# Choice sums moved into the first expert stage, normalisations given to ScalarE, and exponent differences given to TensorE

## The chip, the cores and the metric
The kernel runs on one core of a Trainium2 chip. The metric is the device time of one execution in microseconds (us). All data are float32 unless said otherwise.

## The reference
4096 rows (64 sequences of 64 positions) of 256 features pass through four residual steps, each behind a tanh gate:

```
x = x + tanh(g_xattn[0]) * attention(layernorm(x), ctx)          # 16 x 16 heads within a position
x = x + tanh(g_ffn[0])   * experts0(layernorm(x))                # 16 experts, 6 chosen, plus a shared one
x = x + tanh(g_xattn[1]) * wkv(layernorm(x) as keys, ctx as values)
x = x + tanh(g_ffn[1])   * experts1(layernorm(x))                # 64 experts, 8 chosen
```

The third step, the mixing, is a recurrence over the 64 positions for each feature, with w the decay and u the bonus:

```
no = max(o, u + k); A = exp(o - no); E = exp(u + k - no); y = (A*p + E*v) / (A*q + E)
no2 = max(w + o, k); A2 = exp(w + o - no2); E2 = exp(k - no2); p, q, o = A2*p + E2*v, A2*q + E2, no2
```

## The kernel before
The 4096 rows are 32 tiles of 128 rows, in 8 groups (NG) of four tiles (GT). x_res holds all rows on chip. Each engine has a program of its own, in order, and the engines meet at semaphores and at the ends of the stages A, B, G0, H0, M, H1, I1 (end_stage: every engine drains and waits for all).

- A and B are the attention, G0 the first routing. G0 writes each normalised row once for each chosen expert to a DRAM table (xs_a), sorted by expert.
- H0 (`experts(L0)`, `slots(L0)`) runs 208 tiles of 128 sorted rows through their experts. At step j TensorE turns the rows of tile j, multiplies tile j-1 by its first weights (L920), turns the hidden rows of tile j-2 (L928) and multiplies tile j-3 by the second weights (L937). VectorE adds the bias of tile j-1 (h_gu, L1649), waits for ScalarE's gate (h_sg, L1153), multiplies (h_h, L1655), scales tile j-3 (h_y, L1664), and in every fourth step compares, picks and places the row numbers. GpSimd scatters h_y to y_a, where the six results of a row lie side by side.
- M (`over_time` and what stands around it) does in group order: sum the six results of each row (`choices_summed` on TensorE, L978, from k_a loaded by SyncE, `choices_added` on VectorE, L1735), the statistics (`moments_of`), normalise to keys (`keys`, L1747), turn them, a scan over time for the largest exponent (`exponents`, L1762), the maximum (L1764), four differences (L1765 to L1769), their exponentials on ScalarE (`decays`, L1212 to L1214), scans and products (`over_time`, twice, for the two halves of the features, called chunks), the division (`divided`, L1796, L1801), the residual (`residual`, L1806), and the second routing (`normalised_rows`, `less_largest`, `chosen_experts`, `slots_of`), which lags one group behind. GpSimd issues 32 indirect transfers a group (L646), once `slots_of` has given their rows. The order of all this on each engine is written out by hand in loops over g = 0..8. SyncE loads weights of the second layer behind the last choices (`weights1`).
- H1 is like H0, for 320 tiles of the second layer. From step 103 on it also sums the eight results of rows already done, in four parts at four consecutive steps for a token tile (`token_in` on SyncE, `add_token` on VectorE, L1680 to L1689); a token tile follows every 8 steps. I1 does this for the last group.

The steps at which sums stand come from a table that is made when the kernel is built:

```
sum_at = {}
for t in range(NT - GT):
    ready = tiles_of_groups(t // GT + 1) + SUM_ROOM
    sum_at[t] = ready + (8 if t // GT < NG - 2 else 6) * (t % GT)
```

Of the kernel before, what the change touches and what calls it, by code (L numbers as in the profile page):

```python
# [69 lines left out]
def flamingo(nc, x, ctxT, gates, wqkvT, bqkv, woT, bo, gate0T, gate0b, exp0, exp0b, sh1T, sh3T, sh2T, shb, bs2,  # L70
# [10 lines left out]
    with ctx:  # L81
# [106 lines left out]
        with ExitStack() as st:  # L188
# [19 lines left out]
            h_gu = s_("h_gu", [P, 2, 2 * L0.H])  # L208
            w_bias = s_("w_bias", [P, L0.E * 2 * L0.H])
# [4 lines left out]
        with ExitStack() as st:  # L214
# [8 lines left out]
            w_o = s_("w_o", [P, GB, SEQ + 1])  # L223
            w_t = s_("w_t", [P, KC, 4, GB, SEQ])
# [4 lines left out]
            w_max = s_("w_max", [P, GB, SEQ])  # L229
# [7 lines left out]
            k_a = s_("k_a", [P, 2, GT // 2, L0.K * D])  # L237
# [94 lines left out]
        wk_e = sem("wk_e")  # L332
# [7 lines left out]
        wk_std = sem("wk_std")  # L340
        wk_xn = sem("wk_xn")
        wk_tr = sem("wk_tr")
        wk_k = sem("wk_k")
        k_in = [sem(f"k_in{s}") for s in range(2)]
# [15 lines left out]
        logit_bank = {"a": 2, "b": 6}  # L360
        rank_bank = {"a": 3, "b": 7}
        done = {"a": 0, "b": NG}

        def tiles_of_groups(n):
            return NTOK // NG * L1.K // P * n + L1.E - 1
# [20 lines left out]
        def _(sp):  # L386
# [106 lines left out]
            def token_in(t):  # L493
                if t % GT == 0:
                    n = tiles_of_groups(t // GT + 1)
                    for s in range(YB):
                        sp.wait_ge(lay["b"]["y_st"][s], 16 * ((n - s + YB - 1) // YB))
# [10 lines left out]

            def token_out(t):
                sp.dma_start(out_v[t], s_x[:, t % 2]).then_inc(out_st, 16)  # L510

            def slots(L):
# [5 lines left out]
                if L is L1:  # L518
                    for t, step in sum_at.items():
                        load_at.setdefault((step - SUM_ROOM + 3) // HB + nb - 1, []).append(t)  # L520
                n = L.tiles // HB
                for m in range(max(n, max(load_at, default=0) + 1)):
# [5 lines left out]
                    for t in load_at.get(m, []):  # L528
                        token_in(t)
# [5 lines left out]

            def choices_in(g):
                for h in range(2):
                    if g:
                        sp.wait_ge(k_done, 2 * g - 1 + h)
                    sp.dma_start(k_a[:, h], y_of[g, :, 2 * h:2 * h + 2, 0:L0.K * D]).then_inc(k_in[h], 16)  # L540
# [11 lines left out]
            choices_in(0)  # L552
# [3 lines left out]
            choices_in(1)  # L556
            context_in(1)
            sp.dma_start(e_g1[:], gate1T.rearrange("(c p) n -> p c n", p=P)).then_inc(gate1_in, 16)
            for g in range(NG):
                if g + 2 < NG:  # L560
                    choices_in(g + 2)
# [4 lines left out]
            sp.wait_ge(k_done, 2 * NG)  # L566
            weights1(weight_parts[0])
# [134 lines left out]
        def _(pe):  # L702
# [269 lines left out]
            def choices_summed(g):  # L972
                for h in range(2):
                    pe.wait_ge(k_in[h], 16 * g + 16)
                    if g:
                        pe.wait_ge(k_used, g)
                    for k in range(L0.K):
                        m = pe.matmul(ps[:, 2 + h, :], ident[:], k_a[:, h, :, k * D:(k + 1) * D],  # L978
                                      start=(k == 0), stop=(k == L0.K - 1))
                    m.then_inc(k_done, 1)  # L980
# [18 lines left out]
            choices_summed(0)  # L999
            keys_turned(0)  # L1000
            pe.wait_ge(gate1_in, 16)
            for g in range(NG + 1):
                if g:
                    states_back(g - 1)
                if g + 1 < NG:
                    choices_summed(g + 1)
                if g:
                    turned(L1, g - 1)
                    logits(L1, g - 1, e_g1)
                    ranks(L1, g - 1)  # L1010
                if g + 1 < NG:
                    keys_turned(g + 1)
            experts_of_tiles(L1, 2)
# [7 lines left out]
        def _(act):  # L1021
# [177 lines left out]
            def key_deviations(g):  # L1199
                act.wait_ge(wk_var, g + 1)  # L1200
                part = slice(g * GT, g * GT + GT)
                act.activation(rstd[:, part], mean_v[:, part], ACT.Sqrt).then_inc(wk_std, 1)

# [6 lines left out]
            def decays(g, c):  # L1210
                act.wait_ge(wk_t, 2 * g + c + 1)
                act.activation(w_a2[:, c, :, 1:SEQ + 1], w_t[:, c, 0], ACT.Exp, bias=w_wu[:, c:c + 1])  # L1212
                act.activation(w_e2[:, c, :, 1:SEQ + 1], w_t[:, c, 1], ACT.Exp)
                act.activation(w_ex[:, c].rearrange("p j b t -> p (j b t)"),  # L1214
                               w_t[:, c, 2:4].rearrange("p j b t -> p (j b t)"), ACT.Exp).then_inc(wk_e, 1)

            key_deviations(0)
            act.wait_ge(wk_pad, 1)
            keys_turned(0)
            act.wait_ge(wk_in, 32)  # L1220
            for g in range(NG + 1):
                if g < NG:
                    decays(g, 0)
                if g:
                    deviations(L1, g - 1)
                if g < NG:
                    decays(g, 1)
                if g:
                    turned(L1, g - 1)
                    exponentials_of(L1, g - 1)  # L1230
                if g + 1 < NG:
                    key_deviations(g + 1)
# [8 lines left out]
        def _(dve):  # L1241
# [112 lines left out]
            def moments_of(g, ready=None):  # L1354

                part = slice(g * GT, g * GT + GT)
                for t in range(g * GT, g * GT + GT):
                    dve.bn_stats(stats[:, t, :], x_res[:, t, :])
                dve.drain()
# [260 lines left out]
            def experts(L):  # L1620
# [48 lines left out]
                for t, step in sum_at.items():  # L1669
                    for part in range(4):  # L1670
                        adds_at.setdefault(step + part, []).append((t, part))

# [19 lines left out]
                def body(b, first):  # L1692
# [3 lines left out]
                    for s in range(TD):  # L1696
# [14 lines left out]
                        if L is L1:  # L1711
                            for t, part in adds_at.get(j, []):
                                add_token(t, part)
# [19 lines left out]
            def choices_added(g):  # L1733
# [181 lines left out]
```

## Time and profile before
| | us |
|---|---|
| median of 3 runs | 2300.85 (2299.5 to 2301.25) |
| the profiled execution | 2299.31, its span 2297.5 |
| TensorE matmul busy | 1661.1 (72%) |
| VectorE busy | 1335.5 (58%) |
| ScalarE busy | 688.2 (30%) |
| GpSimd busy | 1051.2 (46%) |
| mean granted clock | 0.856 of full |

The times of rows are in us from the start of the span. H0 goes from about 683 to 1230 us, M from 1230 to 1755, H1 from 1755 to 2270. Busy shares are means over stages with different limits, so each stage is to be read by itself. "Idle before" is the time that an engine stood still in front of an instruction, with the one that released it.

### The profile page before, as it was taken

How to read it: one execution, taken by the hardware profiler on the slowest of the kernel's cores; microseconds unless marked ns; L12 is line 12 of the kernel's file. 1: busy time of each engine (PE TensorE's matmuls, PEld its weight loads, DVE VectorE, ACT ScalarE, POOL GpSimd, SP SyncE). 2: the span in 40 equal slices, each digit the busy share in tenths (PEclk: the TensorE clock that was granted, in tenths of full speed). 3: DMA queues.
4: the chain of work that ended last, by engine and by line, in shares of the span. 5: the costliest groups of instructions: out<-in, count | busy, mean ns of one | idle time of the engine just before them, and what ended most of it. 6: DMA issues, size and time to landing. Idle time of an engine off the chain costs nothing. (4 is left out here: it accounts for less than half of the span.)

```text
span 2297.5 us, 36021 instructions
## 1 busy us (share of the span) xinstructions
PE 1661.1 (72%) x9250; PEld 1209.0 (53%) x9250; DVE 1335.5 (58%) x3716; ACT 688.2 (30%) x1894; POOL 1051.2 (46%) x1039
## 2 busy tenths in 40 slices
PE   2959984987609999999994433333113999999993
PEld 1437763654307777777772222222113888787872
DVE  5113323666505555555552999999951567777774
ACT  1421221222003333333330322222202555455541
POOL 5022001677743333333331056666674666566662
PEclk9989995998859999999996766666556999999997
DMA  4585736533435576675524344442595668788885
GB/s 145 183 147 71 95 68 225 203 122 113 149 128 187 185 257 207 222 239 189 190 84 144 128 139 159 160 162 96 192 339 171 189 193 268 258 279 275 291 270 180
DMA packets 245364, 419.25 MB, mean 182 GB/s; under 512 B 92097, under 2 KB 176193, under 8 KB 243265
## 3 DMA queue, kind: packets, MB, share of 16 engines
q1 hardware_dynamic: 172336, 215.58, 33.1%
q0 software_dynamic: 48144, 138.57, 16.3%
q10 hardware_dynamic: 24704, 62.98, 7.9%
q8 instruction: 78, 1.28, 0.2%
q14 instruction: 102, 0.83, 0.1%
HBM read 253.36 MB, written 209.88 MB: 202 GB/s over the span
## 5 line engine op out<-in xcount | busy, mean ns | idle before, releaser
L920 PE MATMUL ps<-w_all,h_xT 128*128 x2112 | 547.7, 382 | 5.1 <-ACT h_xT L1143 5.1
L937 PE MATMUL ps<-w_all,h_hT 89*128 (+1 forms) x1472 | 416.2, 387 | 2.5
L663 POOL DMA_INDIRECT y_b<-h_y,h_ix x320 | 316.5, 989 | 203.9 <-DVE h_y L1664 105.9
L646 POOL DMA_INDIRECT xs_b<-h_x,slot_of x256 | 270.9, 1058 | 243.8 <-DVE slot_of L1497 167.9
L920 PEld LDWEIGHTS ps<-w_all,h_xT 128*128 128x128 f32 x2112 | 344.2, 191 | 53.9 <-issue 9.4
L663 POOL DMA_INDIRECT y_a<-h_y,h_ix x208 | 201.3, 968 | 350.8 <-DVE h_y L1664 341.6
L913 PE MATMUL ps<-ident,h_x 128*128 128x128 f32 x1056 | 204.6, 275 | 119.4 <-DMA h_x<-xs_a 63.6
L1664 DVE TENSOR_SCALAR h_y<-ps,h_sum 128x256 f32<-128x256 f32 x528 | 253.5, 480 | 49.0 <-PE ps L937 24.9
L937 PEld LDWEIGHTS ps<-w_all,h_hT 89*128 89x128 f32 (+1 forms) x1472 | 239.1, 191 | 32.5 <-issue 7.1
L1143 ACT COPY h_xT<-ps 128x256 f32<-128x256 f32 x528 | 195.8, 371 | 166.9 <-PE ps L913 148.3
L913 PEld LDWEIGHTS ps<-ident,h_x 128*128 128x128 f32 x1056 | 149.2, 142 | 176.5 <-issue 120.1
L646 POOL DMA_INDIRECT xs_a<-h_x,slot_of x192 | 189.4, 986 | 106.0 <-issue 57.9
L928 PE MATMUL ps<-ident,h_h 128*88 128x128 f32 (+1 forms) x736 | 170.3, 278 | 11.4 <-DVE h_h L1655 8.8
L1153 ACT ACTIVATE h_sg<-h_gu 128x176 f32<-128x176 f32 x208 | 72.8, 350 | 324.5 <-DVE h_gu L1649 324.5
L1158 ACT COPY h_hT<-ps 96x128 f32<-96x128 f32 (+1 forms) x528 | 154.3, 292 | 14.1 <-PE ps L928 9.3
L1649 DVE TENSOR_TENSOR h_gu<-ps,w_bias 128x352 f32<-128x352 f32 x208 | 109.0, 524 | 80.8 <-PE ps L920 57.8
L928 PEld LDWEIGHTS ps<-ident,h_h 128*88 128x88 f32 (+1 forms) x736 | 91.0, 124 | 92.8 <-issue 40.1
L1655 DVE TENSOR_TENSOR h_h<-ps,h_sg 128x96 f32<-128x96 f32 x320 | 81.6, 255 | 94.7 <-ACT h_sg L1153 91.5
L1655 DVE TENSOR_TENSOR h_h<-h_gu,h_sg 128x176 f32<-128x176 f32 x208 | 71.1, 342 | 107.1 <-ACT h_sg L1153 107.1
L861 PE MATMUL ps<-h_y,e_w 128*128 128x512 f32 (+1 forms) x192 | 98.1, 666 | 27.4 <-DVE e_h L1569 27.1
L978 PE MATMUL ps<-k_a,ident 128*128 128x512 f32 x192 | 95.7, 660 | 19.2 <-DMA k_a<-y_a 19.2
L1153 ACT ACTIVATE h_sg<-ps 128x96 f32<-128x96 f32 x320 | 80.1, 250 | 94.2 <-PE ps L920 93.7
(237 smaller groups left out, 2143.9 us busy)
## 6 DMA issues: line engine op xcount, KB each, us to landing
xs_b<-void_d ACTq DMA_DIRECT2D x40, 1128.0 KB, 13.7
h_x<-xs_b SPq DMA_DIRECT2D x80, 564.0 KB, 7.6
h_x<-xs_a SPq DMA_DIRECT2D x52, 564.0 KB, 4.2
k_a<-y_a SPq DMA_DIRECT2D x16, 1536.0 KB, 7.9
w_all<-in_exp SPq DMA_DIRECT2D x7, 2560.0 KB
h_x<-y_b SPq DMA_DIRECT2D x28, 512.0 KB, 4.7
s_b<-y_b SPq DMA_DIRECT2D x28, 512.0 KB
qkv_d<-a_out ACTq DMA_DIRECT2D x8, 1536.0 KB, 7.5
```

Source lines behind the costliest of these rows:

```text
L646: pool.indirect_dma_start(xs_d[L.name], bass.IndirectOffsetOnAxis(ap=slot_of[:, g * GT + j, k:k + 1], axis=0), h_x[:, g % NB, j, :], None) ...
L663: pool.indirect_dma_start(y_d[L.name], bass.IndirectOffsetOnAxis(ap=h_ix[:, s:s + 1], axis=0), h_y[:, s % YB, :], None).then_inc(q["y_st"] ...
L913: m = pe.transpose(ps[:, s % 2, c * P:(c + 1) * P], h_x[:, i // HB % nb, s % HB, c * P:(c + 1) * P], ident[:])
L920: m = pe.matmul(ps[:, 2 + s % 2, 0:2 * L.H], h_xT[:, s % 2, c, :], w_all[:, bass.ds(e * L.W + c * 2 * L.H, 2 * L.H)], start=(c == 0), stop ...
L928: m = pe.transpose(ps[0:h1, 4 + s % 2, j * P:(j + 1) * P], h_h[:, s % 2, j * h1:(j + 1) * h1], ident[:])
L937: m = pe.matmul(ps[:, 6 + s % 2, 0:D], h_hT[0:w, s % 2, j, :], w_all[0:w, bass.ds(e * L.W + L.up0 + j * D, D)], start=(j == 0), stop=(j == ...
L1143: act.copy(h_xT[:, s % 2].rearrange("p c n -> p (c n)"), ps[:, s % 2, 0:D])\
L1153: act.activation(h_sg[:, s % 2, 0:L.H], src, ACT.Silu).then_inc(q["s_done"], 1)
L1158: act.copy(h_hT[0:h1, s % 2, 0:L.NC, :].rearrange("p j n -> p (j n)"), ps[0:h1, 4 + s % 2, 0:L.NC * P]).then_inc(q["ht_ready"], 1)
L1649: dve.tensor_tensor(h_gu[:, s % 2, :], ps[:, 2 + s % 2, 0:2 * L.H], w_bias[:, bass.ds(e * 2 * L.H, 2 * L.H)], ALU.add).then_inc(q["b_done" ...
L1655: dve.tensor_tensor(h_h[:, s % 2, 0:L.H], src, h_sg[:, s % 2, 0:L.H], ALU.mult)\
L1664: dve.tensor_scalar(h_y[:, s % YB, :], ps[:, 6 + s % 2, 0:D], h_sum[:, s // HB, s % HB, 0:1], None, ALU.mult)\
```

## The change
1. The choice sums of the first seven groups (28 token tiles) leave M and go into H0: SyncE loads a token tile's six results (h_c) between the row loads, and VectorE adds them in parts at consecutive steps. With the last tile of a group the moments follow. The token tiles stand 6 steps apart, in the last of the seven groups 4. The last group is summed in M as before, from a k_a loaded at once.
2. In M, `keys` and the four multiplications of `normalised_rows` leave VectorE. ScalarE does them as Identity with a scale and a bias of each row; VectorE only makes the reciprocal and the bias, for 28 tiles of keys at once.
3. The four differences leave VectorE. TensorE adds a with the identity and -b with a negated identity into one of three PSUM banks, and ScalarE takes the exponential from there, four instructions a chunk in place of three.
4. The orders in M change: both chunks' differences stand together on TensorE, both chunks' exponentials together on ScalarE in front of the deviation, and on VectorE the reciprocals and the division come ahead of the slots.

```diff
-        sum_at = {}
-        for t in range(NT - GT):
-            ready = tiles_of_groups(t // GT + 1) + SUM_ROOM
-            sum_at[t] = ready + (8 if t // GT < NG - 2 else 6) * (t % GT)
+        sum_at = {"a": {}, "b": {}}
+        for L in (L0, L1):
+            each = NTOK // NG * L.K // P // GT
+            for t in range(NT - GT):
+                ready = tiles_of_groups(L, t // GT + 1) + SUM_ROOM
+                sum_at[L.name][t] = ready + (each if t // GT < NG - 2 else each - 2) * (t % GT)
...
+            def first_token_in(t):
+                if t % GT == 0:
+                    n = tiles_of_groups(L0, t // GT + 1)
+                    for s in range(YB):
+                        sp.wait_ge(lay["a"]["y_st"][s], 16 * ((n - s + YB - 1) // YB))
+                if t:
+                    sp.wait_ge(t_done, t)
+                sp.dma_start(h_c[:], of_tokens(L0)[t // GT, :, t % GT, 0:L0.K * D]).then_inc(t_in, 16)
...
+            def differences(g, c):
+                o_prev, o_now = w_o[:, c, :, 0:SEQ], w_o[:, c, :, 1:SEQ + 1]
+                key, largest = w_k[:, c, :, 1:SEQ + 1], w_max[:, c]
+                pe.wait_ge(wk_t, 2 * g + c + 1)
+                for v, (a, b) in enumerate(((o_prev, o_now), (key, o_now), (o_prev, largest), (key, largest))):
+                    n = 4 * (2 * g + c) + v
+                    if n >= 3:
+                        pe.wait_ge(wk_exp, n - 2)
+                    pe.matmul(ps[:, spread[n % 3], :], ident[:], a, start=True, stop=False)
+                    pe.matmul(ps[:, spread[n % 3], :], minus[:], b, start=False, stop=True).then_inc(wk_less, 1)
...
             for g in range(NG + 1):
                 if g:
                     states_back(g - 1)
-                if g + 1 < NG:
-                    choices_summed(g + 1)
+                if g < NG:
+                    differences(g, 0)
+                    differences(g, 1)
                 if g:
                     turned(L1, g - 1)
                     logits(L1, g - 1, e_g1)
-                    ranks(L1, g - 1)
+                if g == 0:
+                    last_choices_summed()
                 if g + 1 < NG:
                     keys_turned(g + 1)
+                if g:
+                    ranks(L1, g - 1)
...
+            def scaled(g, dst):
+                for j in range(GT):
+                    t = g * GT + j
+                    m = act.activation(dst[:, j, 0:D], x_res[:, t, :], ACT.Identity, bias=mean[:, t:t + 1],
+                                       scale=rstd[:, t:t + 1])
+                return m
...
                 if g < NG:
                     decays(g, 0)
+                    decays(g, 1)
                 if g:
                     deviations(L1, g - 1)
-                if g < NG:
-                    decays(g, 1)
-                if g:
+                    rows_normalised(g - 1)
                     turned(L1, g - 1)
                     exponentials_of(L1, g - 1)
...
+                def first_add_token(t, part):
+
+                    if part == 0:
+                        dve.wait_ge(t_in, 16 * t + 16)
+                        dve.tensor_tensor(h_c[:, 0:3 * D], h_c[:, 0:3 * D], h_c[:, 3 * D:6 * D], ALU.add)
+                    elif part == 1:
+                        dve.drain()
+                        dve.tensor_tensor(h_c[:, 0:D], h_c[:, 0:D], h_c[:, D:2 * D], ALU.add)
+                        dve.drain()
+                        dve.tensor_tensor(h_c[:, 0:D], h_c[:, 0:D], h_c[:, 2 * D:3 * D], ALU.add)
+                    elif part == 2:
+                        dve.drain()
+                        dve.scalar_tensor_tensor(x_res[:, t, :], h_c[:, 0:D], tgate[:, 2:3], x_res[:, t, :],
+                                                 ALU.mult, ALU.add).then_inc(t_done, 1)
+                    elif part == 3:
+                        dve.drain()
+                        dve.bn_stats(stats[:, t, :], x_res[:, t, :])
+                    else:
+                        moments_from_stats(t // GT, wk_var if t == NT - GT - 1 else wk_part)
...
-                dve.tensor_tensor(w_t[:, c, 0], o_prev, o_now, ALU.subtract)
-                dve.tensor_tensor(w_t[:, c, 1], key, o_now, ALU.subtract)
-                dve.drain()
-                dve.tensor_tensor(w_t[:, c, 2], o_prev, w_max[:], ALU.subtract)
-                dve.scalar_tensor_tensor(w_t[:, c, 3], key, u, w_max[:], ALU.add, ALU.subtract).then_inc(wk_t, 1)
...
                 if g < NG:
                     exponents(g, 1)
-                if g:
-                    normalised_rows(L1, g - 1)
-                if g < NG:
                     over_time(g, 0)
                 if g:
+                    row_scales(g - 1)
+                if g < NG:
+                    over_time(g, 1)
+                if g == 0:
+                    last_choices_added()
+                if g == 2:
+                    key_scales(2, slice(NT - GT, NT))
+                if g < NG:
+                    denominators(g)
+                if g:
                     less_largest(L1, g - 1)
-                if g + 1 < NG:
-                    choices_added(g + 1)
+                if g < NG:
+                    divided(g)
                 if g:
                     chosen_experts(L1, g - 1)
-                if g < NG:
-                    over_time(g, 1)
-                if g:
                     slots_of(L1, g - 1)
-                if g + 1 < NG:
-                    keys(g + 1)
-                if g < NG:
-                    divided(g)
```

SyncE's loads in M shrink accordingly: `weights1(weight_parts[0])`, the first part of the second layer's weights, moves from behind the last choices to the third round of its loop.

## Rows read from the trace of the kernel before

**Rows 1.** Windows, VectorE's L1664 alone: us, busy (tiles), clock, DMA share, GB/s
```profile
740.00:1180.00 440.00, 82.86 (x173) 1.00 0.62 206
1770.00:1890.00 120.00, 40.13 (x83) 1.00 0.65 190
2010.00:2210.00 200.00, 61.01 (x127) 1.00 0.85 282
```

**Rows 2.** Waits of VectorE, 740 to 1180 us: total, times, longest
```profile
DVE h_gu L1649 <- PE ps L920: 46.4, 92, 0.9
```

**Rows 3.** Groups of instructions, VectorE's additions in H1: busy, mean ns, idle before
```profile
L1683 DVE TENSOR_TENSOR h_x<-h_x,s_b 128x512 f32<-128x512 f32 x28 | 19.4, 694 | 2.1
...
L1689 DVE SCALAR_TENSOR_TENSOR s_x<-h_x,tgate,s_x 128x256 f32<-128x256 f32 x28 | 14.6, 520 | 4.6 <-issue 4.5
...
L1685 DVE TENSOR_TENSOR h_x<-h_x 128x256 f32<-128x256 f32 x28 | 11.9, 427 | 2.1
```

**Rows 4.** Timeline, one iteration of M on VectorE: start, duration
```profile
1405.46 1.24 DVE L1762 TENSOR_TENSOR_SCAN w_o<-w_dec,w_k 128x520 f32<-128x520 f32 x1
1406.79 0.75 DVE L1764 SCALAR_TENSOR_TENSOR w_max<-w_k,w_wu,w_o 128x512 f32<-128x512 f32 x1
...
1410.09 1.28 DVE L1806 SCALAR_TENSOR_TENSOR x_res<-ps,tgate,x_res 128x1024 f32<-128x1024 f32 x1
...
1413.98 1.24 DVE L1762 TENSOR_TENSOR_SCAN w_o<-w_dec,w_k 128x520 f32<-128x520 f32 x1
...
1418.59 0.25 DVE L1377 COPY h_x<-tail 128x40 f32<-128x40 f32 x1
...
1420.47 0.74 DVE L1778 TENSOR_TENSOR w_ev<-w_e,w_v 128x512 f32<-128x512 f32 x1 [0.16 <-issue]
...
1427.72 1.27 DVE L1735 SCALAR_TENSOR_TENSOR x_res<-ps,tgate,x_res 128x1024 f32<-128x1024 f32 x1
...
1429.09 1.41 DVE L1358 BATCH_NORM_STATS2 stats<-x_res 128x6 f32<-128x256 f32 x4
...
1431.49 0.41 DVE L1403 TENSOR_REDUCE r_t<-r_p 128x4 f32<-128x256 f32 x1
...
1436.81 0.69 DVE L1778 TENSOR_TENSOR w_ev<-w_e,w_v 128x512 f32<-128x512 f32 x1
...
1443.20 0.21 DVE L1461 TENSOR_TENSOR r_cnt<-r_cnt,ps 128x64 f32<-128x64 f32 x1
...
1449.93 0.17 DVE L1743 RECIPROCAL rstd<-rstd 128x4 f32<-128x4 f32 x1
...
1451.76 6.57 DVE L1796 RECIPROCAL w_d<-w_d 128x512 f32<-128x512 f32 x2
...
1459.78 1.24 DVE L1762 TENSOR_TENSOR_SCAN w_o<-w_dec,w_k 128x520 f32<-128x520 f32 x1
```

**Rows 5.** Timeline: M's first instruction, slots of group 6, and H1's first instruction
```profile
1230.52 0.11 DVE L1552 MEMSET r_cnt<- 128x64 f32 x1 [11.76 <-POOLq L381]
...
1663.79 0.18 DVE L1497 TENSOR_SCALAR slot_of<-r_sl 128x32 int32<-128x32 f32 x1
...
1755.49 1.28 ACT L1182 ACT_TABLE_LOAD   x1 [67.23 <-POOLq L381]
```

**Rows 6.** Windows of L978 (clock after PEld); L978 in the timeline; ScalarE's groups
```profile
1297.00:1300.00 3.00, 1.12 (x2) 0.81 (x3) 0.50 0.00 0
1303.00:1306.00 3.00, 3.00 (x8) 1.33 (x7) 1.00 0.00 0
...
1409.69 9.18 PE L978 MATMUL ps<-k_a,ident 128*128 128x512 f32 x21
...
L1098 ACT ACT_TABLE_LOAD x16 | 20.5, 1283 | 18.8 <-DVE mean_v L1368 18.5
...
L1212 ACT ACTIVATE w_a<-w_t,w_wu 128x512 f32<-128x512 f32 x16 | 11.6, 723 | 83.2 <-DVE w_t L1769 83.2
```

**Rows 7.** DMA issues: KB each, us to landing
```profile
k_a<-y_a SPq DMA_DIRECT2D x16, 1536.0 KB, 7.9
```

More of the change, by code:

```diff
@@ L236, in flamingo @@
             w_end = nc.sbuf_base
-            k_a = s_("k_a", [P, 2, GT // 2, L0.K * D])
+            k_a = s_("k_a", [P, GT, L0.K * D])
             assert nc.sbuf_base <= nc.sbuf_top - big, (nc.sbuf_base, nc.sbuf_top - big)
@@ L343, in flamingo @@
         wk_k = sem("wk_k")
-        k_in = [sem(f"k_in{s}") for s in range(2)]
+        k_in = sem("k_in")
         k_done = sem("k_done")
@@ L517, in slots @@
                 load_at = {}
-                if L is L1:
-                    for t, step in sum_at.items():
-                        load_at.setdefault((step - SUM_ROOM + 3) // HB + nb - 1, []).append(t)
+                for t, step in sum_at[L.name].items():
+                    load_at.setdefault((step - SUM_ROOM + 3) // HB + nb - 1, []).append(t)
                 n = L.tiles // HB
@@ L555, in _ @@
             context_in(0)
-            choices_in(1)
+            sp.dma_start(k_a[:], y_of[NG - 1, :, :, 0:L0.K * D]).then_inc(k_in, 16)
             context_in(1)
@@ L1354, in moments_of, with moments_from_stats @@
             def moments_of(g, ready=None):
-                part = slice(g * GT, g * GT + GT)
                 for t in range(g * GT, g * GT + GT):
                     dve.bn_stats(stats[:, t, :], x_res[:, t, :])
+                moments_from_stats(g, ready)
+            def moments_from_stats(g, ready):
+                part = slice(g * GT, g * GT + GT)
                 dve.drain()
@@ L1668, in experts @@
                 adds_at = {}
-                for t, step in sum_at.items():
-                    for part in range(4):
+                for t, step in sum_at[L.name].items():
+                    for part in range(4 if L is L1 or t % GT < GT - 1 else 5):
                         adds_at.setdefault(step + part, []).append((t, part))
+                def first_add_token(t, part):
[14 more added lines that the diff above has]
+                        dve.bn_stats(stats[:, t, :], x_res[:, t, :])
+                    else:
+                        moments_from_stats(t // GT, wk_var if t == NT - GT - 1 else wk_part)
                 def add_token(t, part):
@@ L1710, in body @@
                             place_of(s // HB)
-                        if L is L1:
-                            for t, part in adds_at.get(j, []):
-                                add_token(t, part)
+                        for t, part in adds_at.get(j, []):
+                            (first_add_token if L is L0 else add_token)(t, part)
                 dve.memset(h_oh[:], 1.0)
```

134 lines of the change are left out of this document (76 added, 58 removed).

## The prediction
> **What bounds the kernel now.** I read the page's forty slices first, to cut the span into its stages, then for each of the two stages that the change touches the view that says which engine never waits. In the first expert stage (H0) the windows view gives 173 tiles in 440 us, 2.54 us each, at the full TensorE clock [rows 1], and VectorE's waits for TensorE are the only idle time of VectorE that other work could fill: 46.4 us over those 173 tiles, 0.27 us a tile [rows 2]. Its other gaps (for ScalarE's gate between two of its own instructions, for register reads and drains) stand inside its chain and can't be filled, since the engine works in order. So TensorE sets the tile, with VectorE 0.27 us behind it. In the mixing stage (M) one iteration on VectorE goes from scan to scan in 54.3 us, 1405.46 to 1459.78, and the steps of the timeline follow one another without a wait [rows 4]: VectorE is the bound until its last slots but one (1663.79). GpSimd then has two groups to dispatch, and 91.7 us later the next stage starts (1755.49) [rows 5].
>
> **H0: what is added.** 28 tokens' tiles are summed there, four parts each, and seven fifth parts. Prices: a 512-wide addition is 0.694 us and a 256-wide one 0.427 [rows 3], which makes a 768-wide one 0.96, less about 0.08 by which an instruction starts before the end of one that it doesn't depend on: 0.88. A drain costs 0.09 (scan 1405.46 plus 1.24, the next at 1406.79) [rows 4]. Part 1, two 256-wide additions with two drains, is 1.0. Part 2, 0.52 with its drain [rows 3], is 0.60. Part 3, one of the four statistics that take 1.41 [rows 4], taken as 0.40 with its overhead, is 0.48. Together 2.96 a token, 82.9 for 28. Part 4, the small moments, is the time from 1429.09 plus 1.41 to 1431.49 [rows 4], 1.0, and a drain: 7.5 for seven. Sum 90.4 us.
> What hides it: the 161 tiles from step 47 to 207 have 0.27 us each, 43 us. A delay of VectorE can be carried from tile to tile only a little (h_h is wanted by the next but one transposition), so nothing more is hidden, and the cycle of gate, product and result turns into the bound: 90.4 - 43 = 47 us. Both ends: 0 if all of it were hidden, 90 if none. I take 47, since VectorE's order is fixed.
> SyncE issues 28 token loads between the row loads. A token load waits for the token before it (part 2), that is until about step +3; the nearest transfer, a k_a load of 1536 KB, lands in 7.9 us [rows 7], a load of half that in some 5 to 6, two tiles; it is wanted at +6, and the row loads behind it are twelve tiles ahead. Only the last group's tokens stand 4 steps apart; three waits of 0.7 us, 2 us. H0 becomes 49 us longer.
>
> **M: what is taken from an iteration.** Choices and their moments, 1427.72 to 1431.49, 3.8 us; keys, 1449.93 to 1451.76, 1.8; the four differences of a chunk, from the end of the maximum (1406.79 plus 0.75) to 1410.09, 2.6, twice, 5.2; of the normalised rows, 1418.59 to 1420.47 (1.9), 0.7 stays: 1.2 [rows 4]. 54.3 - 12.0 = 42.3 us of work.
> **What it adds are waits.** (a) TensorE makes the differences: per chunk 8 products, 16 instructions. The choice sums had the same shape; 21 take 9.18 us, 0.43 each [rows 6], so a chunk takes 6.9 us at full clock and 13.8 at half. The granted clock is 0.50 in the 3 us in which such a burst starts and 1.00 six us later [rows 6]; TensorE will have been idle some 6 us before the chunk, so the first 4 us run at half: 8.9 us. Chunk 0 starts at 2.1 after the first scan, ends at 11.0, its last exponential (0.72 [rows 6]) at 11.9. VectorE comes there at 2 + 3.9 + 2 = 7.9 (residual 1410.09 to 1413.98) [rows 4]: it waits 4.1. (b) Chunk 1 ends at 17.9, its exponential at 18.7; ScalarE then loads the table for the square root, 1.28 [rows 6], and takes the root: 20.2. VectorE, after 6.4 us of over_time (1436.81 to 1443.20) [rows 4], is at row_scales at 18.3: it waits 1.9. ScalarE's four normalisations, the turn and the logits that hang on them end some 9 us later, beside over_time of chunk 1 and the 6.6 us of reciprocals: no wait. The keys of the next group are normalised on ScalarE after the routing's exponential, at 35 to 37, and turned by 40, eight us before they are wanted: what hides them is the choice of experts and the slots. The iteration is 42.3 + 6.0 = 48.2 us. Bounds of the two waits together: 0 if TensorE is at full clock and ahead of the scans, 17 if all differences run at half.
> **Its start and end.** Group 0's sums, moments and deviation no longer stand in front. From the stage's start at 1230.5 [rows 5] the table load, root and scales (2), four normalisations (2), transposes at half clock and two copies (3.5) make 7.5 us to the first scan. Iteration 0 has no routing; work of 26 us, a wait of 8 for chunk 0, and about 6 for the last group's sums, 24 instructions of 0.43 that come behind all differences: 40. In the new order the reciprocals and the division stand ahead of the slots, so slots come at the iteration's end; slots of group 6 at 1230.5 + 7.5 + 40 + 7 x 48.2 = 1615.4, and with the same 91.7 us behind them [rows 5] (GpSimd's 41 us a group are less than 48.2, so no backlog; the last slots are ready 27 us on) the stage ends at 1707.1 in place of 1755.5: 48.4 us shorter. The weight loads of the second layer start as far ahead of that end as before, some 90 us. H1, G0 and the rest don't change.
> **Sum.** 2299.31 (the profiled execution, span 2297.5) + 49 - 48.4 = 2299.9. The median of the runs shown is 1.5 us above the profiled execution, so 2301 us against 2300.85: no change. The gain of one stage is paid in the other, because VectorE is the second bound in H0 by 0.27 us only.
>
> **Rivals.** *The sums hide in H0 as they do in H1.* H1 sums its tokens the same way: 83 tiles in 120 us before the sums begin, 127 in 200 with them [rows 1], 1.446 and 1.575 us, 0.13 x 8 = 1.0 us a token, for some 3.0 us of added work by the same prices: a third. A third of 90.4 is 31, so 18 us less: 2283. For it: it is the same helper pattern. Against: in H1 VectorE has more open time in a tile, the gate is read from PSUM without an addition in front.
> *The differences come late (the slower side).* If the clock doesn't rise within chunk 0, the chunk takes 13.8 in place of 8.9, VectorE waits 4.9 us more in each of eight iterations: 39 us, 2340. It decides from the point where TensorE's idle time before chunk 0 is long and the ramp takes over 5 us. For it: the clock is 0.50 at each start of a burst. Against: 1.00 at 1303, six us after [rows 6]. The Trainium skill (TensorE: Matmul & The Clock Gate, Part 1: The HAM clock gate) says that the lower clock is the default and that sustained activity releases it; by that rule the same loss follows if the new gaps keep the engine in its default, and the trace's two levels in rows 6 agree with the rule, not with how long this kernel needs.
> *Token loads late.* If each token waits 1 us for its load, for the void stores share the DMA engines: 28 us, 2329.
> *The waits in M vanish* (6 us by 8): 2253.
>
> **Numbers.** Forecast 0.53, of its own range 2290 to 2313; hidden sums 0.18; late differences 0.13; late loads 0.11; no waits 0.05. 2 in 10 left out give 2274 to 2336. A measurement tells 0.2%, 4.6 us, from nothing. Faster: 0.17 of the forecast, 0.18 and 0.05: 0.40. Same: 0.20. Slower: 0.16, 0.13 and 0.11: 0.40.
>
> **What would show it.** In the profile after, H0 must be 49 us longer, with VectorE's waits for TensorE at L1649's successor near zero and TensorE waiting for h_h; right if the tile is 2.5 us up to step 47 and 2.8 behind. In M the first scan must stand 7.5 us behind the stage's start, scans 48 us apart, with waits of 4 us for the exponentials and 2 us for the deviation. The forecast is wrong if H0 grows by under 35 us, if an iteration is outside 46 to 51 us, or if the DMA wait of a token's first part is seen more than a few times.

## The result and the profile after

The changed kernel takes 2325.12 us (median of 4 runs, 2319.38 to 2328.53), the kernel before, beside it, 2300.18 (2298.6 to 2301.25): 1.0106 times the time, with an interval of 1.0082 to 1.0131. It is slower by 1%. The profiled execution took 2319.38, its span 2317.6, 20.1 us more than the span before. By stages, H0 from VectorE's first instruction in it, M from SyncE's load of w_wu (in the kernel before 0.9 us behind the first instruction of the stage), H1 from ScalarE's table load, each to the next:

| stage | before | after | difference | forecast |
|---|---|---|---|---|
| H0 | 551.3 | 617.6 | +66 | +49 |
| M | 524.1 | 480.7 | -43.4 | -48.4 |
| H1 | 521.7 | 519.8 | -2 | 0 |

**H0.** Windows of the changed kernel, VectorE's L1713 alone, the line that was L1664 [rows 1]: us, busy (tiles), clock, DMA share, GB/s.
```profile
740.00:820.00 80.00, 14.86 (x31) 1.00 0.69 232
820.00:1240.00 420.00, 67.95 (x142) 0.97 0.64 217
900.00:940.00 40.00, 5.74 (x12) 0.87 0.64 218
```
The sums begin at 805 us. In the first window a tile takes 2.58 us (2.54 in [rows 1]), in the second 2.96, and in the worst stretch 3.3. What VectorE waited for from 740 to 1297 us (total, times, longest):
```profile
DVE h_c L1726 <- DMA h_c<-y_a: 28.2, 7, 8.3
DVE h_gu L1698 <- PE ps L930: 12.9, 30, 0.9
```
The second line is that of [rows 2], 46.4 us there: most of the open time is filled. The first is new. It says that the first addition of a token tile stood in front of a load that hadn't landed, seven times, up to 8.3 us. The timeline of one of them, VectorE's and two queues' (ACTq and SPq are the queues of ScalarE and SyncE):
```profile
896.41 0.47 ACTq L1187 DMA_DIRECT2D xs_b<-void_d  x1
896.92 1.93 ACTq L1187 DMA_DIRECT2D xs_b<-void_d  x3
898.49 0.33 SPq L526 DMA_DIRECT2D h_c<-y_a  x1
916.47 0.96 DVE L1726 TENSOR_TENSOR h_c<-h_c 128x768 f32<-128x768 f32 x1 [8.22 <-DMA h_c<-y_a]
```
ScalarE's queue issues four void stores of 1128 KB within 3 us, and SyncE's queue then a token load of 768 KB. It lands and is used 18 us later; the median from issue to landing of these loads is 4.6. The trace has the landing of all 28: the five that were issued 0.3 to 6.6 us behind a burst took 12.6 to 18.4 us, the other 23, at least 16.8 us behind one, 4.4 to 5.8. Those five make 26.5 of the 28.2 us; the other two waits, 1.7 us together, are in the last group, where the token tiles stand 4 steps apart. While VectorE waits, so do the gate and product of the tiles, and TensorE for them; its granted clock falls to half at four of these waits (913.2 to 923.5 us is the longest stretch). The Trainium skill (DMA: Bandwidth & Descriptors, Issuing engines are not separate DMA queues) says that transfers issued from different engines run on the same 16 DMA engines and interleave there; this trace agrees, with 18 us behind a burst against 4.6.

**M.** Its first instruction, the first scan, the wait of the first iteration, and TensorE's at the same place:
```profile
1296.80 0.33 SPq L564 DMA_DIRECT2D w_wu<-in_wkv_w  x1
...
1303.13 1.24 DVE L1836 TENSOR_TENSOR_SCAN w_o<-w_dec,w_k 128x520 f32<-128x520 f32 x1 [1.57 <-ACT w_k L1245]
...
1321.72 0.69 DVE L1848 TENSOR_TENSOR w_ev<-w_e,w_v 128x512 f32<-128x512 f32 x1 [14.35 <-ACT w_ex L1258]
```
```profile
1311.70 2.08 PE L998 MATMUL ps<-w_o,ident 128*128 128x512 f32 x2 [9.72 <-DMA e_g<-in_gate1T]
```
TensorE's order has the wait for the routing gate's weights (e_g, 64 KB) ahead of the first difference, and they were issued behind the 3072 KB of the last group's choices. One later iteration on VectorE, which answers to [rows 4]:
```profile
1446.73 1.24 DVE L1836 TENSOR_TENSOR_SCAN w_o<-w_dec,w_k 128x520 f32<-128x520 f32 x1 [0.16 <-issue]
...
1458.57 0.69 DVE L1848 TENSOR_TENSOR w_ev<-w_e,w_v 128x512 f32<-128x512 f32 x1 [3.59 <-ACT w_ex L1258]
...
1466.95 0.18 DVE L1810 RECIPROCAL rstd<-rstd 128x4 f32<-128x4 f32 x1 [1.83 <-ACT rstd L1120]
...
1494.98 1.24 DVE L1836 TENSOR_TENSOR_SCAN w_o<-w_dec,w_k 128x520 f32<-128x520 f32 x1 [0.16 <-issue]
```
48.25 us, with a wait of 3.59 for the exponentials and of 1.83 for the deviation. The end, as in [rows 5]:
```profile
1685.93 0.18 DVE L1546 TENSOR_SCALAR slot_of<-r_sl 128x32 int32<-128x32 f32 x1
...
1777.48 1.28 ACT L1204 ACT_TABLE_LOAD   x1 [76.58 <-POOLq L391]
```

### The profile page after: what moved, and what is told of

The parts are those of the page before. It is cut to its first block and busy times, and to the rows that moved or that the text cites. A ratio compares the mean times of both kernels' runs of the same rounds, so it can differ in the third digit from the quotient of the medians.

```text
span 2317.6 us, 36381 instructions
## 1 busy us (share of the span) xinstructions
PE 1733.8 (75%) x9338; PEld 1229.7 (53%) x9338; DVE 1321.6 (57%) x3698; ACT 710.9 (31%) x1956; POOL 1059.2 (46%) x1039
## 5 line engine op out<-in xcount | busy, mean ns | idle before, releaser
L947 PE MATMUL ps<-w_all,h_hT 89*128 (+1 forms) x1472 | 422.4, 392 | 3.8 <-issue 3.1
L673 POOL DMA_INDIRECT y_a<-h_y,h_ix x208 | 209.9, 1009 | 409.6 <-DVE h_y L1713 404.6
L1713 DVE TENSOR_SCALAR h_y<-ps,h_sum 128x256 f32<-128x256 f32 x528 | 253.4, 480 | 48.1 <-PE ps L947 24.4
L938 PE MATMUL ps<-ident,h_h 128*88 128x128 f32 (+1 forms) x736 | 173.5, 282 | 51.5 <-DVE h_h L1704 48.1
L938 PEld LDWEIGHTS ps<-ident,h_h 128*88 128x88 f32 (+1 forms) x736 | 84.9, 125 | 151.4 <-DVE h_h L1704 113.9
L758 PE MATMUL ps<-k_diag,q_pad 128*32 128x128 f32 x1024 | 84.7, 517 | 19.6 <-DMA q_pad<-qkv_d 19.6
```

What stands on the lines that cost most here:

```text
L673: pool.indirect_dma_start(y_d[L.name], bass.IndirectOffsetOnAxis(ap=h_ix[:, s:s + 1], axis=0), h_y[:, s % YB, :], None).then_inc(q["y_st"] ...
L938: m = pe.transpose(ps[0:h1, 4 + s % 2, j * P:(j + 1) * P], h_h[:, s % 2, j * h1:(j + 1) * h1], ident[:])
L947: m = pe.matmul(ps[:, 6 + s % 2, 0:D], h_hT[0:w, s % 2, j, :], w_all[0:w, bass.ds(e * L.W + L.up0 + j * D, D)], start=(j == 0), stop=(j == ...
L1713: dve.tensor_scalar(h_y[:, s % YB, :], ps[:, 6 + s % 2, 0:D], h_sum[:, s // HB, s % HB, 0:1], None, ALU.mult)\
```

## The experiments

They ran on three chips, and these differ: the kernel before takes 2490.23 us on the first (experiments 1 to 4), 2489.44 on the second (5 to 8), and 2300.89 on the third (9 to 12). Whole times, M and H1 are compared within a chip only. H0 is within some 3 us on all of them, so it is compared across chips too: the kernel before has 551.3 in its own trace and 550.7 on the third chip, the changed kernel 617.6 and 614.5 on the second. The first chip has no trace of either; there H0 of the changed kernel with single stores is 578.6, and with the same H0 578.0 on the second.

**1. One void store at a time.** In H0 of the changed kernel ScalarE issues one void store every four tiles.
```diff
-                    if voids_too:
-                        for v in range(EACH):
-                            void_slots(EACH * (b - 1) + v)
                     for s in range(TD):
                         j = TD * b + s
+                        if voids_too and s % (TD // EACH) == 0:
+                            void_slots(EACH * (b - 1) + s // (TD // EACH))
```


> The changed kernel, but ScalarE issues its 40 stores of empty rows in H0 one at a time every four tiles in place of four together every sixteen. Theory A (H0's 66 us are about 38 us of VectorE's sums with the clock that falls on them and 28 us of waits for token loads that meet a burst of these stores): the seven waits of 28.2 us in all fall under 8 us, the granted clock stays full in H0, H0 is 20 to 28 us shorter than in the changed kernel, the whole about 2298. Rival B (a token load is late because it is asked for late, behind part 2 of the token before, whatever else the DMA engines do): the waits stay about 28 us in all, spread over more tokens, and the time stays at 2320 to 2328.

2485.23 us (10 runs) against 2490.23 for the kernel before: 0.9974 (0.9956 to 0.9993). The loads are issued at the same steps as before. VectorE's waits for them in H0 (total, times, longest):
```profile
DVE h_c L1725 <- DMA h_c<-y_a: 0.6, 2, 0.4
```
H0 is 578.6 us, with the full clock up to its last 15 us: 36 less than the 614.5 of the changed kernel, more than the 20 to 28 of theory A. The loads weren't asked for late; the stores in front of them made them late. So rival B falls.

**2. One token load.** The first token is loaded, all additions stay and work on it (so the sums aren't those of the reference), the stores come in bursts.
```diff
-                if t:
-                    sp.wait_ge(t_done, t)
-                sp.dma_start(h_c[:], ...
+                if t == 0:
+                    sp.dma_start(h_c[:], ...
```


> The changed kernel with one token load in place of 28 in H0: all additions and moments of VectorE stay, but act on what the one load brought, so the sums are not the rows'. Theory A: H0 (549.8 us from 747 us of the stage's wait, here from its first tile to the next stage's start 613 us after against 547 before) grows by 38 us over before in place of 66. Rival C (VectorE's added work alone explains the growth, by the serial account of the prediction 47 us, and the lower clock the rest): 47 to 66 us. If the sums hide as they do in H1: 31 us.

2489.37 us, a single run. H0 584.2: the added work of VectorE alone, with the bursts, costs 584.2 - 550.7 = 34 us. Theory A said 38, rival C 47 to 66, and sums that hide as in H1 31.

**3. No additions.** Loads and their waits stay; additions, residual and statistics of the 28 tokens are left out, so those rows lack the first layer's expert sums.
```diff
-                        dve.tensor_tensor(h_c[:, 0:3 * D], h_c[:, 0:3 * D], h_c[:, 3 * D:6 * D], ALU.add)
...
-                        dve.scalar_tensor_tensor(x_res[:, t, :], h_c[:, 0:D], ...).then_inc(t_done, 1)
+                        dve.sem_inc(t_done, 1)
```

> The changed kernel with all 28 token loads and VectorE's waits for them in H0, but without the additions, the residual and the statistics of these 28 tiles, which are left out. Theory A: H0 grows by 20 to 28 us over before, in some five waits of 3 to 8 us that lie in the bursts of the stores of empty rows. Rival C: by 0 to 5 us.

2487.14 us, a single run. H0 585.4; the waits are there without any of the work:
```profile
DVE h_gu L1698 <- DMA h_c<-y_a: 35.5, 9, 6.9
```
The waits alone cost 585.4 - 550.7 = 35 us, more than the 20 to 28 of theory A. 34 and 35 together are a little more than the 64 to 66 that H0 grew.

**4. Scaled result on ScalarE.** In H0 ScalarE makes h_y, with the gate as its scale, three tiles behind the turn; VectorE's L1713 is left out there.
```diff
+                def result(i, s, used):
+                    ...
+                    act.activation(h_y[:, s % YB, :], ps[:, 6 + s % 2, 0:D], ACT.Copy,
+                                   scale=h_sum[:, s // HB, s % HB, 0:1]).then_inc(q["y_done"], 1)
```


> The changed kernel with the scaled results of H0 (h_y, 0.48 us a tile) moved from VectorE to ScalarE, which is 36% busy there. Theory A with the serial account: VectorE gets 0.4 us a tile back, more than the 0.3 us by which the sums exceed its open time, so only the 28 us of load waits and their clock are left: H0 35 to 40 us shorter than in the changed kernel, the whole about 2287, under the kernel before. Rival D (ScalarE now stands in the chain, its copy of the turned rows and its gate come later): H0 no shorter, 2320 or more.

2503.77 us (10 runs), 1.0044 (1.0023 to 1.0065). H0 597.1, 17 us less than the changed kernel's 614.5, with the bursts as they were. Neither end was right: theory A had 35 to 40 us less, rival D nothing. VectorE has time again, and spends it in front of the loads:
```profile
DVE h_c L1742 <- DMA h_c<-y_a: 41.2, 11, 9.2
```

**5. The changed kernel, on the second chip**, unchanged.

> The changed kernel once more, beside the kernel before, as the control on this chip. All theories: its ratio to the kernel before is that of the first measurement, 1.008 to 1.013, and the token sums of H0 wait 28 to 41 us for their loads. If the ratio is under 1.004, the chip decides and not the kernel.

2523.01 us (4 runs), 1.014 (1.0113 to 1.0168), H0 614.5, M 522.6, H1 581.0; 26.9 us of load waits, a little under the 28 to 41 expected. The ratio is just above that of the first measurement (1.0082 to 1.0131), with the same cause in sight.

**6. The kernel before with single void stores**, the edit of experiment 1 alone.

> The kernel before with one thing changed: in H0 the void stores go out one at a time, every four tiles, and not four together every sixteen. Theory (the stores harm only the loads of the token sums): nothing in the kernel before waits for a transfer in H0, so it stays as it is, within 0.1%. Rival (the stores in bursts cost every kernel something, and spreading them is a gain of its own): this kernel is faster by 0.2% or more, and the gain of spreading in the changed kernel isn't the removal of its waits alone.

2481.76 us (12 runs), 0.9966 (0.995 to 0.9982): the rival was right. Windows of 20 us of the kernel before (third chip) and of this one: us, busy (instructions) of TensorE, weight loads, VectorE, ScalarE, GpSimd, then clock, DMA share and GB/s.
```profile
880.00:900.00 20.00, 19.56 (x95) 14.41 (x94) 11.46 (x32) 6.75 (x24) 7.64 (x8) 1.00 0.76 260
900.00:920.00 20.00, 20.00 (x98) 14.79 (x97) 11.70 (x33) 7.12 (x26) 7.82 (x9) 1.00 0.59 192
```
```profile
880.00:900.00 20.00, 20.00 (x99) 14.81 (x98) 11.76 (x32) 7.40 (x26) 7.53 (x9) 1.00 0.64 221
```
With bursts TensorE has idle time in every other window up to 1120 us; with single stores it has none between 780 and 1280. H0 is 541.4 against 550.7. The traces show by which wait. One burst in the kernel before (third chip), on ScalarE and its queue, and TensorE behind it:
```profile
886.57 0.48 ACTq L1165 DMA_DIRECT2D xs_b<-void_d  x1
...
887.08 1.91 ACTq L1165 DMA_DIRECT2D xs_b<-void_d  x3
889.08 0.37 ACT L1143 COPY h_xT<-ps 128x256 f32<-128x256 f32 x1 [1.99 <-issue]
...
889.68 1.45 PE L920 MATMUL ps<-w_all,h_xT 128*128 x4 [0.44 <-ACT h_xT L1143]
```
And TensorE's waits for that copy from 720 to 1120 us (total, times, longest):
```profile
PE ps L920 <- ACT h_xT L1143: 4.6, 9, 0.8
```
ScalarE starts no new work while it issues the four stores, 0.6 us each, so its copy of the turned rows comes 2 us late and TensorE's next product waits for it. TensorE stands still like this at each of the ten bursts, 5.0 us in all (the tenth, 0.43 us, the profile puts down to "issue"); with single stores TensorE never waits for this copy. From the first gate addition to the one 176 tiles on, the kernel with bursts takes 7.1 us more. So the waits go back to ScalarE's time for issuing, and not to bandwidth: no engine waits for a row load in these windows; the other 2 lie before the first of these tiles and behind the last, and with two chips compared their cause isn't shown.

**7. Single void stores, and the gate's weights first.**
```diff
             context_in(0)
+            sp.dma_start(e_g1[:], ...).then_inc(gate1_in, 16)
             sp.dma_start(k_a[:], y_of[NG - 1, ...
             context_in(1)
-            sp.dma_start(e_g1[:], ...).then_inc(gate1_in, 16)
```


> The changed kernel with two edits: void stores of H0 spread, and the routing gate's weights of the mixing loaded ahead of the 3072 KB of the last group's choices. Theory: H0 loses the 28 us of load waits and some 8 us of halved clock (35 us less than the changed kernel); in M the first iteration loses most of TensorE's wait of 9.7 us for the weights, of which 6 reach the end: together 1.5 to 1.8% less than the changed kernel, ratio to the kernel before 0.992 to 0.997. Rival (the wait for the weights is only exchanged for a wait for the choices, which come later by the same bytes): the first iteration stays at 47 us and the ratio is that of spreading alone, 0.997.

2474.86 us (6 runs), 0.9946 (0.9925 to 0.9967). H0 578.0, 36.5 us less than the changed kernel on this chip; M 515.0, 7.6 less, and the first iteration, scan to scan, 40.3 against 48.1. Theory right on both: 35 and 6 were forecast, and the ratio lies in its range.

**8. The same, and the scaled result on ScalarE.**

> As the kernel with both edits, and in H0 the scaled result (h_y) is made by ScalarE, as in H1 it is by VectorE still. Theory (with the load waits gone, VectorE's 90 us of added work bounds H0, less its 43 us of open time): ScalarE takes 173 instructions of some 0.4 us off VectorE, 60 to 70 us, more than the 38 us that H0 is still too long, so H0 comes back to the kernel before's length and the kernel is 1 to 1.6% faster than without the third edit. Rival (ScalarE is in the same chain gate, product, result, and each tile's result now waits in its order behind the turn and the gate of later tiles): H0 stays the same within 5 us or grows, as far as ScalarE's own 0.4 us a tile isn't hidden.

2433.7 us (6 runs), 0.9782 (0.9758 to 0.9806), 1.7% less than experiment 7. H0 541.2, 36.8 less than in experiment 7 and as long as in experiment 6, where no sums are. TensorE's weight loads waiting for VectorE's product, 745 to 1345 us in experiment 7 (of the 65.8 us, 64.2 lie behind 840) and 840 to 1313 here:
```profile
PEld ps L938 <- DVE h_h L1703: 65.8, 99, 2.8
```
```profile
PEld ps L938 <- DVE h_h L1719: 11.4, 31, 2.0
```
The same edit was worth 17 us under the bursts and 37 without: two causes in one stage, and the second showed its full size once the first was gone.

**9. The kernel before, on the third chip**, unchanged.

> The kernel before once more, for its trace beside those of the other kernels of this chip. Theory (bursts of void stores take bandwidth from H0 of every kernel, which the kernel with single void stores gives back): H0 some 8 us longer than that kernel's 541, M 556 and H1 591 as there. Rival (the 0.34% of spreading come from elsewhere, a later or an earlier stage): H0 within 3 us of 541, and another stage longer.

2302.0 us, a single run. H0 550.7, M 524.1, H1 523.0. H0 is 9.2 longer than with single stores; 8 was forecast, and the gain of 0.34% (8.4 us at 2489) lies there. The theory's reason, bandwidth, isn't what the trace shows (experiment 6). That M and H1 would be 556 and 591 was wrong: they belong to the second chip.

**10. Experiment 7 without the token sums' work** (the loads stay, the rows lack the sums).

> The changed kernel with void stores spread and the gate's weights first, and the 28 token sums in H0 left out with their residual and statistics (the loads stay, so the output lacks the first layer's expert sums of seven groups). H0 was 578.0 us with the sums on this kind of chip. Theory (VectorE's 90 us of work less 43 of open time, 47): H0 531 to 541 us, as long as the kernel before's. Rival (a third of the work shows, as H1's sums do, 31 us): 547. Second rival (the loads alone, 21 MB more in H0, cost bandwidth of the row loads): above 555.

2245.22 us, a single run. H0 542.0; with the work it was 578.0: VectorE's added work is worth 36 us, between the theory's 47 and the rival's 31 and nearer to the rival. The second rival, that the loads themselves cost bandwidth, falls: 21 MB more, and H0 is as long as in experiment 6 without them. M is 476.5.

**11. First chunk's differences on VectorE again**, written straight into the PSUM tiles that ScalarE reads; the rest as experiment 8.
```diff
+            def less_on_vector(g, c):
+                ...
+                    dve.tensor_tensor(ps[:, spread[n % 3], :]..., a, b, ALU.subtract).then_inc(wk_less, 1)
...
                     exponents(g, 0)
+                    less_on_vector(g, 0)
...
-                    differences(g, 0)
                     differences(g, 1)
```


> The fastest kernel so far (void stores spread, gate weights first, scaled result of H0 on ScalarE: ratio 0.978 to the kernel before, M 516.8 us), with the four differences of the first chunk of channels made by VectorE again, straight into the PSUM tiles that ScalarE reads, and those of the second chunk by TensorE as before. Theory (the differences on TensorE only turn VectorE's work into a wait of the same size): VectorE does 2.6 us more an iteration and no longer waits 3.6 to 4.1 for the first chunk's exponentials, 1.2 us less in each of eight: M 507, ratio 0.974. Rival (the writes wait for ScalarE to free the three tiles, 0.7 us each, and TensorE's clock falls further): M 517 to 525, ratio 0.978 to 0.982.

2253.24 us (5 runs), 0.9794 (0.9777 to 0.9811). M 486.9, against 476.5 in experiment 10, whose M is the same program as the changed kernel's with the weights first: 10 us worse. The ratio falls into the rival's range. Of its two reasons the waits for the three tiles hardly occur (one of 0.89 us in the whole of M); the clock does fall further. One iteration takes 50.4 us (1370.05 to 1420.49) instead of 47.9; TensorE's clock is at its lower level for 44.4 us around it (1342.0 to 1386.4), in experiment 10 for 30.7 an iteration. Its timeline:
```profile
1378.52 1.24 DVE L1852 TENSOR_TENSOR_SCAN w_o<-w_dec,w_k 128x520 f32<-128x520 f32 x1
...
1380.64 2.07 PE L998 MATMUL ps<-w_o,ident 128*128 128x512 f32 x2 [15.71 <-DVE w_max L1854]
...
1390.64 0.69 ACT L1272 ACTIVATE w_ex<-ps,w_wu 128x512 f32<-128x512 f32 x1 [1.12 <-PE ps L999]
1391.34 1.28 ACT L1119 ACT_TABLE_LOAD   x1
1392.64 0.21 ACT L1119 ACTIVATE rstd<-mean_v 128x4 f32<-128x4 f32 x1
1392.88 0.18 DVE L1826 RECIPROCAL rstd<-rstd 128x4 f32<-128x4 f32 x1 [5.57 <-ACT rstd L1119]
```
The wait for the exponentials is gone, and the one for the deviation has grown from 1.8 to 5.6: TensorE now comes to the second chunk after 15.7 us without work, runs its first half at half clock (0.50 from 1381 to 1384, 1.00 from 1387), and ScalarE has the deviation's square root behind the last exponential of that chunk. In the changed kernel the second chunk follows at once on the first, whose end runs at the higher clock already.

**12. Both chunks' differences on VectorE.**
```diff
                     exponents(g, 1)
+                    less_on_vector(g, 1)
...
-                    differences(g, 1)
```

> The same with the differences of both chunks made by VectorE, none by TensorE: what the third part of the change is worth by itself. Theory: the second chunk's exponentials are wanted only after the first chunk's sums over time, so nothing waited for them; VectorE does 2.6 us more and may save some of the 1.3 to 1.9 us that it waits for the deviation: M 507 + 8 times 0.7 to 2.6, 513 to 528, ratio 0.977 to 0.983. Rival (the differences on TensorE are worth their 5.2 us of VectorE work, their waits being there anyway): M 517 + 8 times 5.2, 558, ratio 0.995.

2233.4 us (5 runs), 0.9707 (0.9691 to 0.9724): the fastest of all, and neither end was forecast. M 466.4. From one iteration:
```profile
1359.71 1.24 DVE L1850 TENSOR_TENSOR_SCAN w_o<-w_dec,w_k 128x520 f32<-128x520 f32 x1 [0.16 <-issue]
...
1361.88 0.70 DVE L1863 TENSOR_TENSOR ps<-w_o 128x512 f32<-128x512 f32 x1
...
1372.88 0.69 ACT L1270 ACTIVATE w_ex<-ps,w_wu 128x512 f32<-128x512 f32 x1
1373.01 0.69 DVE L1873 TENSOR_TENSOR w_ev<-w_e,w_v 128x512 f32<-128x512 f32 x1 [0.16 <-ACT w_ex L1268]
...
1379.48 0.17 DVE L1824 RECIPROCAL rstd<-rstd 128x4 f32<-128x4 f32 x1
```
VectorE does eight instructions of 0.7 us more, started 0.61 apart, and hardly waits (no wait from 1264 to 1600 us is over 0.4 us): 47.5 us an iteration (1359.71 to 1407.20) against 47.9 in experiment 10. The first iteration is 35.5 (1228.81 to 1264.29) against 41.5 (1231.11 to 1272.64), where VectorE waited 8.87 for its first exponentials. TensorE's clock is at its lower level throughout (0.50 from 1375 to 1471), and VectorE doesn't wait for it.

## Why the prediction was right or wrong

**The number.** Forecast 2301, measured 2325.12, inside the range of 2274 to 2336. But the range was wide enough for the rivals, and the likeliest case isn't what happened: that was the rival of late token loads, with its mechanism (the void stores share the DMA engines), its 28 us and its 2329. The chance given to it was 0.11. Its form is another, though, five long waits and not 1 us a token, and that 2325 comes so near its 2329 is in part luck: H0's work is 11 to 13 us less than forecast, its load waits 26 to 28 more, M 5 longer. By the prediction's own signs it is wrong on one point: the wait of a token's first part is seen seven times. What counted against it was thought to be room in time ("the row loads behind it are twelve tiles ahead"), and that says nothing of what else is in the queues.

**H0, VectorE's work: the right mechanism, a term too large.** Forecast 47. Measured 34 under the bursts (experiment 2) and 36 without them (578.0 less 542.0, experiments 7 and 10, on two chips). That is nearer to the rival's 31, which took the share that shows from H1, than to the forecast. (The rival's 2283 takes off 18 us; 47 less 31 is 16, so its sum should be 2285.) Two windows of all H0 show the work, with it (experiment 7) and without (experiment 10); VectorE's busy time is the third pair.
```profile
773.00:1348.00 575.00, 542.89 (x2494) 378.73 (x2494) 373.97 (x1020) 189.59 (x625) 210.30 (x208) 0.98 0.64 217
```
```profile
686.00:1225.00 539.00, 522.99 (x2496) 384.21 (x2496) 303.53 (x832) 190.01 (x626) 201.47 (x213) 0.99 0.70 233
```
70.4 us more busy, and 34.5 less idle (235.5 to 201.0): that is the 36. The idle time in front of the gate's addition, with the work and without:
```profile
DVE h_gu L1697 <- PE ps L930: 17.4, 31, 4.2
DVE h_gu L1697 <- issue: 14.2, 36, 0.8
```
```profile
DVE h_gu L1697 <- PE ps L930: 52.9, 93, 4.2
DVE h_gu L1697 <- issue: 23.9, 64, 0.7
```
35.5 and 9.7 us filled, 45.2 in all, against the 43 of the forecast. That they agree is partly luck: the 43 counted waits for TensorE alone, of which 35.5 went, and the 9.7 are of the gaps that the prediction said can't be filled. What was too high is the price: 70.4 busy and 13.3 idle between the additions (the groups' idle time before them, summed) are 84, not 90.4; which of the prices was too dear isn't parted here. The last 3 us may be the small waits for rows and loads (3.0 and 1.6) that only the kernel without the work shows. The gap behind ScalarE's gate stayed, as forecast: 84.0 us in 170 waits with the work, and 18.5 in 38 more that the profile puts down to "issue"; 103.2 in 208 without. Whoever reads the first line alone would think that 19 us of it were filled. That VectorE was the engine that decided is shown by experiment 8: with one instruction a tile taken off it, all 37 us went.

**H0, load waits: the step that failed.** "Three waits of 0.7 us, 2 us", from a transfer that lands in 7.9 us, halved [rows 7]. That price was read in M, where no void store runs, and outside the bursts it is right: 4.4 to 5.8 us to landing, and 1.7 us of waits in the last group. Behind a burst it isn't: 12.6 to 18.4 us, and 26.5 us of waits. In all 28.2 us in seven pieces; 30 us from the work alone to the changed kernel (614.5 less 584.2); 35 by themselves (experiment 3); 0.6 with single stores (experiment 1). That single stores gave back 36 us and not 30 fits with experiment 6: the bursts hold up ScalarE too, some 7 us. The trace of before had the bursts: 4 times 1128 KB every 40 us, which at the 260 GB/s of the window at 880 us are some 18 us of transfers (an estimate), as long as the worst load took.

**M, an iteration: right.** Forecast 48.2 with waits of 4.1 and 1.9; measured 46.95 to 49.65 for the six behind the first, 48.0 in the mean, with waits of 2.71 to 4.80 and 1.83. The two windows of TensorE in which this stands, at the first differences of an iteration (us, busy, clock, DMA share, GB/s):
```profile
1448.00:1452.00 4.00, 3.14 (x4) 0.50 0.76 293
1452.00:1456.00 4.00, 4.00 (x10) 0.93 0.45 168
```
The rival of late differences fell: the clock is up within the first chunk. The Trainium skill (TensorE: Matmul & The Clock Gate, Part 1: The HAM clock gate) calls the lower clock the default, released by sustained activity; these windows and experiment 11 agree.

**M, start and end.** First scan 6.3 us after the stage's start, forecast 7.5. Tail (from the slots of group 6 to H1) 91.6, forecast 91.7. Six iterations from the second scan on: 288.1 us against 325.3, 37.2 less, forecast 36.6. What failed is iteration 0: 47.0, forecast 40. The wait for e_g stood in TensorE's order ahead of the first difference, behind a transfer of twice the size of [rows 7]; it isn't in the forecast at all. With the weights first it is 40.3 (experiment 7) and 41.5 (experiment 10).

**What the parts are worth, by the runs.** Sums moved into H0: they cost H0 64 to 66 us, 36 once the stores are spread, and nothing once ScalarE makes the scaled result (the kernel before with that edit alone wasn't run). Differences on TensorE: half a us lost an iteration (48.2 against 47.6, the means of six in experiments 10 and 12), and 6 us in iteration 0; together 10 us of M to the wrong side. M's gain is then left to the sums, the key moments and the normalisations that left VectorE, and to the new order; that is by subtraction, and no run parted these. Experiment 12 keeps them and has 466.4 in place of 524.1.

## What to carry to other kernels

A transfer's landing time holds only beside the traffic in which it was read: before a load goes on the path, list the stores that other engines' queues issue in the same microseconds, and spread a burst before judging the load. A burst costs its issuing engine as well: ScalarE's next copy came 2 us late. An elementwise step moved from the bound engine to TensorE pays what it takes off less the new wait for its results, lower clock included; here 5.2 us were taken off and 5.4 waited. And two causes in one stage hide each other: an edit that buys 17 us beside a stall can be worth 37 without it, so try it again when the stall is gone.

## What wasn't expected of the hardware

VectorE writes a 128x512 difference into PSUM in 0.69 to 0.70 us, as its products into SBUF (0.69). ScalarE starts no copy while its own queue issues stores of 1128 KB, 0.6 us each, though the bytes are moved elsewhere (experiment 6). The chips differ by 190 us with the same program, and not in H0: with single stores it is 541.4 us on the second chip (experiment 6) and 542.0 and 543.0 on the third (experiments 10 and 12). Some 85 us lie ahead of H0, 32 in M and 68 in H1. M is 556.4 us on the second chip for the kernel before with single stores and 524.1 on the third for the kernel before; on the second VectorE has idle times, up to 12.7 us, that end with nothing the profile shows. VectorE's longest "issue" waits in M of these two (total, times, longest), the second chip first:
```profile
DVE r_t L1391 <- issue: 17.5, 4, 12.7
DVE r_m L1435 <- issue: 14.7, 5, 9.1
```
```profile
DVE w_ev L1778 <- issue: 1.6, 8, 0.5
```
What makes the difference stays open.
